# A two-stage layer on one core: small weight parts, a reordered last step, transposes in pairs, last product by halves

## The reference

```python
x = x + attn(layernorm(x))   # proj = x @ W_in * mup; conv over 4 tokens, silu; scan:
    state = state * dA_t + (dt_t * x_t) * B_t ;  y_t = state . C_t
    g = (y + D * x) * silu(z);  g = g * rsqrt(mean(g^2) + eps) * norm_w;  out = g @ W_out
x = x + ffn(layernorm(x))    # g = (x @ gate_w.T) * gate_s; u = (x @ up_w.T) * up_s
    out = ((silu(g) * u) @ down_w.T) * down_s
```

## Time and profile before

| | |
|---|---|
| median of 3 runs | 789.67 us (788.21 to 789.69) |
| the profiled execution | 788.09 us, its span 786.2 us |
| TensorE matmuls busy | 741.8 us (94%) |
| VectorE, ScalarE, POOL busy | 517.7, 494.7, 291.3 us |
| DMA busy (mean of 16 engines) | 41.6% for the program's own queue |
| first stage | 0 to about 523 us |
| second stage | about 526 us to the end |

### The profile page before, as it was taken

How to read it: one execution, slowest core, us unless ns; L and a number is a source line. 1 busy time by engine, 2 the same in 40 slices (tenths; PEclk the granted TensorE clock), 3 DMA queues, 4 the chain that set the end, 5 groups by cost and what they waited for, 6 DMA issues and landing times.

```text
span 786.2 us, 20260 instructions
## 1 busy us (share of the span) xinstructions
PE 741.8 (94%) x8464; PEld 609.7 (78%) x8464; DVE 517.7 (66%) x843; ACT 494.7 (63%) x941; POOL 291.3 (37%) x232
## 2 busy tenths in 40 slices
PE   4877999999999999999999999779999999999997
PEld 4865888888887887887887887567878878887886
DVE  6978976886886887788797796845424532632331
ACT  5988888978977978978978878723312321321330
POOL 2163285375466446546636717420010011001002
PEclk9988999999999999999999999999999999999999
DMA  9833243484484375266367284784013013002002
GB/s 296 232 82 88 47 101 109 100 233 124 83 239 134 85 197 176 79 152 218 84 146 208 71 214 119 254 289 155 0 55 108 0 43 118 0 14 93 0 1 82
DMA packets 42025, 94.94 MB, mean 121 GB/s; under 512 B 9744, under 2 KB 15376, under 8 KB 41744
## 3 DMA queue, kind: packets, MB, share of 16 engines
q1 hardware_dynamic: 41936, 93.67, 41.6%
HBM read 84.73 MB, written 17.57 MB: 130 GB/s over the span
## 4 chain that ended last, share of the span: by engine, by line
PE 51%; DVE 22%; ACT 13%; DMA 6%; issue 5%; POOL 2%; SPq 1%; POOLq 0%; DVEq 0%; ACTq 0%
PE ps_y L1591 10%; DVE cx L895 9%; PE ps_proj L1578 8%; PE ps_out L1578 5%; PE ps_x L1578 5%; PE ps_proj L1174 3%; PE ps_proj L1175 3%; PE ps_proj L1176 3%; ACT ring L678 3%; PE ps_x L1223 3%; DVE ring L950 3%; PE ps_y L1246 2%; DVE dt_p L870 2%; DVE state L960 2%; ACT sz L621 2%
## 5 line engine op out<-in xcount | busy, mean ns | idle before, releaser
L507 POOL TENSOR_TENSOR ring<-tokd,ring 128x1024 f32<-128x1024 f32 x64 | 122.2, 1923 | 187.4 <-ACT tokd L673 125.5
L1174 PE MATMUL ps_proj<-xn_hi,win_hi 128*128 128x256 f32 x608 | 179.0, 294 | 2.7 <-DVE xn_lo L864 2.7
L1175 PE MATMUL ps_proj<-xn_lo,win_hi 128*128 128x256 f32 x608 | 172.9, 284 | 0.0
L1176 PE MATMUL ps_proj<-xn_hi,win_lo 128*128 128x256 f32 x608 | 172.6, 284 | 0.0
L1174 PEld LDWEIGHTS ps_proj<-xn_hi,win_hi 128*128 128x128 f32 x608 | 116.7, 192 | 17.3 <-issue 11.4
L1175 PEld LDWEIGHTS ps_proj<-xn_lo,win_hi 128*128 128x128 f32 x608 | 116.9, 192 | 0.3
L1176 PEld LDWEIGHTS ps_proj<-xn_hi,win_lo 128*128 128x128 f32 x608 | 116.8, 192 | 0.0
L895 DVE SCALAR_TENSOR_TENSOR cx<-cin,consts,cx 128x256 f32<-128x256 f32 x240 | 96.4, 483 | 0.0
L1469 POOL TENSOR_TENSOR res<-res,hidden 128x512 f32<-128x512 f32 x16 | 20.5, 1282 | 184.0 <-DVE hidden L1532 184.0
L950 DVE TENSOR_TENSOR ring<-ring,ps_tok 128x1024 f32<-128x1024 f32 x64 | 75.7, 1215 | 4.2 <-ACT ring L682 4.2
L678 ACT ACTIVATE ring<-ring 128x1024 f32<-128x1024 f32 x64 | 66.7, 1058 | 10.3 <-POOL ring L507 10.3
(11 more groups left out here) (164 smaller groups left out, 1638.1 us busy)
## 6 DMA issues: line engine op xcount, KB each, us to landing
ring<-cum_dram SPq DMA_DIRECT2D x128, 256.0 KB, 5.1
xin<-x SPq DMA_DIRECT2D x8, 512.0 KB, 3.8
res<-x SPq DMA_DIRECT2D x32, 128.0 KB, 2.7
x_dram<-res SPq DMA_DIRECT2D x32, 128.0 KB, 3.2
x_in_sb<-x_dram SPq DMA_DIRECT2D x4, 1024.0 KB, 6.3
res<-x_dram SPq DMA_DIRECT2D x16, 256.0 KB, 2.7
out<-res SPq DMA_DIRECT2D x16, 256.0 KB, 2.0
gate_w_copy<-gate_w SPq DMA_DIRECT2D x4, 704.0 KB, 6.7
```

The costliest lines, as they stand in the source:

```text
L507: pool.tensor_tensor(ring[:, g, :, :], own, ring[:, g, :, :], ALU.subtract).then_inc(diffed, 1)
L1174: pe.matmul(out, win_hi[:, k, cols], xn_hi[:, k, :], start=(k == 0), stop=False)
L1175: pe.matmul(out, win_hi[:, k, cols], xn_lo[:, k, :], start=False, stop=False)
L1176: made = pe.matmul(out, win_lo[:, k, cols], xn_hi[:, k, :], start=False, stop=(k == KT - 1))
```

## The change

1. The weights land in 27 parts: `wg` and `wu` in 8 parts of 352 KB each (128 rows of 704 columns), `wd` in 11 parts of 256 KB. Two on their way at a time as before, and the x1 stores still behind the last part.
2. Tiles 0 and 1 of the first x1 block are loaded one block of the first stage earlier, into the mixer's `xin`, ahead of two weight copies; their statistics and normalisation stand in step 14, their transposes in step 15 right behind `turn_x`.
3. The last step is reordered: `gate_lo(14)` behind `make_xpad`, `scale_carry` ahead of `mix(15, 0)`, the last `skip` made on POOL instead of ScalarE.
4. In `finish` the transposes go in two pairs, one behind t = 0 and one behind t = 1; VectorE's `norm_lo` follows in pairs.
5. The very last tile's product is made in two column halves into two banks; the second half is scaled and added on VectorE (POOL keeps the first) and each half is stored by itself.

```diff
@@ -60,7 +60,8 @@
 BT = 512
 NB = BATCH * LEN // BT
 TT = BT // P
-WEIGHT_PARTS = 2 * KT + 4
+HALF_N = INTER // 2
+WEIGHT_PARTS = 4 * KT + MT
 LOW_WIDTHS = (1024, 1024, 768)
 LOW_EACH = 2 * len(LOW_WIDTHS)
 LOW_PARTS = 3 * LOW_EACH
...
@@ -388,9 +388,11 @@
 
             def body(i, first, last):
                 if i - 1 in LOOKED:
+                    sp.wait_ge(hand.low_max_made, 3 * (i - 2) + 1)
                     if i + 1 < BLOCKS:
-                        sp.wait_ge(hand.low_max_made, 3 * (i - 2) + 1)
                         load_x(i + 1)
+                    else:
+                        sp.dma_start(xin[:], hand.x1_by_block[0, :, 0:2, :]).then_inc(hand.first_in, 16)
                     keep_weights(2 * (i - 2))
                     keep_weights(2 * (i - 2) + 1)
                 if not first:
@@ -432,20 +434,18 @@
                 body(i, False, False)
             body(BLOCKS - 1, False, True)
             sp.wait_ge(projected, EVENTS * BLOCKS)
-            sp.dma_start(hand.xin[:], hand.x1_by_block[0]).then_inc(hand.x_in, 16)
+            sp.dma_start(hand.xin[:, 2:TT, :], hand.x1_by_block[0, :, 2:TT, :]).then_inc(hand.x_in, 16)
             sp.wait_ge(hand.weights_kept, 16 * COPIES)
 
             def load_weights(n):
 
                 if n >= 2:
                     sp.wait_ge(hand.weights_in[n % 2], 16 * (n // 2))
-                if n < KT:
-                    to, part = hand.wg[:, n, :], hand.gate_t[:, n, :]
-                elif n < 2 * KT:
-                    to, part = hand.wu[:, n - KT, :], hand.up_t[:, n - KT, :]
+                if n < 4 * KT:
+                    k, of = n % (2 * KT) // 2, slice(n % 2 * HALF_N, (n % 2 + 1) * HALF_N)
+                    to, part = (hand.wg, hand.wu)[n // (2 * KT)][:, k, of], (hand.gate_t, hand.up_t)[n // (2 * KT)][:, k, of]
                 else:
-                    of = hand.down_parts[n - 2 * KT]
-                    to, part = hand.wd[:, of, :], hand.down_t[:, of, :]
+                    to, part = hand.wd[:, n - 4 * KT, :], hand.down_t[:, n - 4 * KT, :]
                 sp.dma_start(to.bitcast(F32), part).then_inc(hand.weights_in[n % 2], 16)
 
             load_weights(0)
...
@@ -550,6 +564,10 @@
                         fade_state(i, j)
                     if j == 0 and not last:
                         norm_scale(i + 1)
+                    elif j == 0:
+                        mlp_scale(0)
+                    if closing:
+                        last_skip()
                     if not closing:
                         for g in range(GROUPS):
                             if g == GROUPS - 1 and not opening:
@@ -566,11 +584,7 @@
             for i in range(1, BLOCKS - 1):
                 body(i, False, False)
             body(BLOCKS - 1, False, True)
-            pool.wait_ge(hand.zeroed, 2)
-            pool.wait_ge(hand.moments_made, TT)
-            pool.tensor_tensor(hand.spread[:], hand.moments[:, :, 1], hand.eps[:], ALU.add).then_inc(hand.eps_added, 1)
-            pool.wait_ge(hand.eps_added, 1)
-            pool.tensor_tensor(hand.rstd[:], hand.spread[:], hand.minus_half[:], ALU.pow).then_inc(hand.rstd_made, 1)
+            mlp_scale(1)
             fold_squares(STEPS * BLOCKS - 1)
             rms_scale(STEPS * BLOCKS - 1, 1)
             mlp.gpsimd(pool)
...
@@ -751,10 +770,13 @@
                 c = STEPS * i + 1
                 keep_tok(c)
                 fade(c, 0)
-                square(c - 1)
-                if not last:
+                if last:
+                    clamp(c, 2)
+                    square(c - 1)
+                else:
+                    square(c - 1)
                     evacuate(i + 1, 1)
-                clamp(c, 2)
+                    clamp(c, 2)
                 fade(c, 1)
                 if not last:
                     evacuate(i + 1, 2)
@@ -764,8 +786,11 @@
                 if not last:
                     evacuate(i + 1, 3)
                     first_taps(i + 1, CONV_ORDER[0:2])
-                make_skip(i, 1)
-                if not last:
+                if last:
+                    mlp_norm_hi(0)
+                    mlp_norm_hi(1)
+                else:
+                    make_skip(i, 1)
                     first_taps(i + 1, CONV_ORDER[2:4])
                     first_taps(i + 1, CONV_ORDER[4:6])
                     make_run(i + 1)
...
@@ -1010,6 +1028,10 @@
                 if first:
                     weight_lo(EVENTS)
                 update_state(c, 0)
+                if last:
+                    mlp_stats(0)
+                    mlp_normalise(0)
+                    mlp_normalise(1)
                 if first:
                     weight_lo(EVENTS + 1)
                 if not last:
@@ -1027,25 +1049,25 @@
                     all_low_max()
 
                 c = STEPS * i + 1
-                gate_lo(c - 1)
                 if last:
                     mask_cb(c)
                     make_xpad(i, 1)
+                    gate_lo(c - 1)
                     make_x1(c - 2)
-                    mix(c, 0)
-                    mlp_stats()
                     scale_carry(i, 1)
-                    for g in range(1, GROUPS):
+                    for g in range(GROUPS):
                         mix(c, g)
                     make_y(c)
                     gate(i, 1)
-                    mlp_normalise(0)
-                    mlp_normalise(1)
+                    mlp_stats(1)
                     gate_lo(c)
+                    mlp_norm_lo(0)
+                    mlp_norm_lo(1)
                     mlp_normalise(2)
                     mlp_normalise(3)
                     any_low()
                     return
+                gate_lo(c - 1)
                 for n in range(1, 4):
                     soft(i + 1, n)
                 mask_cb(c)
...
@@ -1319,6 +1354,9 @@
                 if not last:
                     project(i + 1, 1)
                 turn_x(i, 1)
+                if last:
+                    mlp_turn(0)
+                    mlp_turn(1)
                 if not last:
                     project(i + 1, 2)
                 carry(i, 1)
...
+                    store_half(j, 0)
+                    store_half(j, 1)
+                else:
+                    store(j, TT - 1)
 
             def store(j, t):
                 sp.wait_ge(out_ready, AHEAD + TT * j + t + 1)
                 sp.dma_start(out_by_block[bass.ds(j, 1), :, t, :].rearrange("a p h -> (a p) h"), res[:, t % 2, :]).then_inc(stored[t % 2], 16)
+
+            def store_half(j, n):
+                t, cols = TT - 1, half_cols(n)
+                if n == 0:
+                    sp.wait_ge(out_ready, AHEAD + TT * j + t + 1)
+                else:
+                    sp.wait_ge(half_ready, 1)
+                sp.dma_start(out_by_block[j, :, t, cols], res[:, t % 2, cols]).then_inc(stored[t % 2], 16)
 
             body(0, True, False)
             with sp.Fori(1, NB - 1) as j:
                 body(j, False, False)
...
@@ -1530,6 +1575,21 @@
                 if t >= 2:
                     dve.wait_ge(out_ready, AHEAD + TT * j + t - 1)
                 dve.tensor_tensor(hidden[:, t % 2, :], ps_o[t % 2], scale_d[:], ALU.mult).then_inc(down_scaled, 1)
+
+            def scale_down_half(j, n):
+
+                t, cols = TT - 1, half_cols(n)
+                dve.wait_ge(down_made, TT * j + t + 1 + n)
+                if n == 0:
+                    dve.wait_ge(out_ready, AHEAD + TT * j + t - 1)
+                made = dve.tensor_tensor(hidden[:, t % 2, cols], ps_last[n], scale_d[:, cols], ALU.mult)
+                if n == 0:
+                    made.then_inc(down_scaled, 1)
+                    return
+                made.then_inc(half_scaled, 1)
+                dve.wait_ge(half_scaled, 1)
+                dve.wait_ge(res_in[t % 2], 16 * (2 * j + t // 2 + 1))
+                dve.tensor_tensor(res[:, t % 2, cols], res[:, t % 2, cols], hidden[:, t % 2, cols], ALU.add).then_inc(half_ready, 1)
 
             def body(j, first, last):
                 for m in range(MT):
...
@@ -1549,12 +1609,19 @@
                         normalise(j + 1)
                 dve.wait_ge(h_split, MT * j + MT)
                 scale_down(j, 0)
+                if not last:
+                    norm_lo(j + 1, 0)
+                    norm_lo(j + 1, 1)
                 scale_down(j, 1)
                 if not last:
-                    for t in range(TT):
-                        norm_lo(j + 1, t)
+                    norm_lo(j + 1, 2)
+                    norm_lo(j + 1, 3)
                 scale_down(j, 2)
-                scale_down(j, 3)
+                if last:
+                    scale_down_half(j, 0)
+                    scale_down_half(j, 1)
+                else:
+                    scale_down(j, 3)
 
             body(0, True, False)
             with dve.Fori(1, NB - 1) as j:
...
@@ -1605,18 +1683,25 @@
             def finish(j, last, exact):
                 pe.wait_ge(h_split, MT * j + MT - 2)
                 down(j, 0, exact)
```

(17 more changed lines are left out.)

92 lines of the change are left out of this document (57 added, 35 removed).

## The result

The changed kernel takes 796.01 us (median of 6 runs, 794.54 to 797.94), the kernel before 788.58 beside it (785.59 to 789.69). The ratio is 1.0103, with a 95% interval of 1.0075 to 1.0131: slower, as forecast, by 7.4 us instead of 3.4, inside the range. The profiled execution took 794.66 with a span of 793.0, against 788.09 and 786.2.

The account below looks back on a forecast made before the run. The hand-over was taken to be bound by how fast SP gets through its list, x1 stores last. Pair 5 +6.6, clock +1.8, transposes -3.1, halves -1.1 on 788.09, plus 0.8 towards the median, gave 793.1 us, range 787.0 to 799.0.

Parts of the forecast that it names:

- the sum: Total against the profiled execution of 788.09: + 6.6 + 1.8 - 3.1 - 1.1 = + 4.2 us.
- the round trips: SP's weight list: each 352 KB part takes r1 = 3.0 us, each 256 KB part r2 = 2.6; bounds 2.4 to 3.5 and 3.0.
- the start of the list: SP: step 13's store lands by 503.1, so weight part 2 is issued at about 504.4 instead of 507.91, 3.5 us earlier.
- over 6 as its sign: Sign that the forecast is right: VectorE waits over 6 us for the second x1 block.
- Early tiles 0 and 1 ... Cost 0: Steps 14 and 15: their work, under 3 us, fits VectorE's 4.59 us wait for PE, transposes PE's wait for `xpad`; cost 0.
- Last step ... gains nothing: Reordered last step: PE ends the first stage 3 to 4 us sooner, about 519.5, but waits for weights until 525.9.
- Clock: PE behind its 7.3 us standstill before pair 5: matmuls at the lower clock cost +1.8 us; bounds 0 and 2.0.
- Transposes: Second stage, transposes in pairs: all 3.2 us of PE's waits go, less 0.1 for more changes: -3.1 us.
- Halves: Last product in two halves: work behind the last matmul shrinks from 2.03 to 1.0 us, quicker half store: -1.1 us.
- The last step late as well: Slower rival: ring loads behind a load and two copies make step 15 1.6 us later, 794.7 us; chance 0.13.
- The small parts at the large parts' rate: Faster rival: round trips shrink with size to 2.4 and 1.8 us, pair 5 at 544.6, total 783.1; chance 0.20.
- the case in between: No-change rival: round trips of 2.7 and 2.5 us and a clock that stays up, 788.7 us; chance 0.17.

Follow-up runs that it names:

- e2: The kernel before with nothing but the 27 small weight parts: 801.36 us, ratio 1.0176.
- e3: The changed kernel, small parts kept, with the x1 stores and the second x1 load ahead of the parts of `wd`: 787.50 us, ratio 1.0012.
- e4: The changed kernel with four small parts on their way instead of two: 780.03 us, ratio 0.9910.
- e12: e10 with the last product still by halves but stored once, in whole rows: 780.01 us, ratio 0.9896.
- e7: e1 with GpSimd held until VectorE's normalisations of the first two and last two rows are done: 779.11 us, ratio 0.9914.
- e1: The changed kernel with the twelve large weight parts of before, all else kept: 779.02 us, ratio 0.9905.
- e11: e10 with GpSimd held by the two waits of e7: 776.12 us, ratio 0.9856.
- e10: Changed kernel, twelve large parts: two before step 13's store, six of `wg`/`wu` at once behind the residual load, x1 stores and load before `wd`: 775.72 us, ratio 0.9857.
- e13: e11 with 48 increments of an unused semaphore on SP behind the last residual load: 775.86 us, ratio 0.9854.
- e6: e1 without the last product by halves (scaled, added and stored whole, as before): 782.45 us, ratio 0.9940.
- e5: The kernel before with only the second stage's transposes in pairs: 782.70 us, ratio 0.9953.

## Why the prediction was right or wrong

*Right: what bounds the kernel, and by what mechanism.* The hand-over hung on SP's list, small parts lengthened it, the x1 stores and pair 5 came late, the clock fell. e2, e3 and e4 show each link. From the issue of part 26 to pair 5 I had 14.4 us, it was 14.3.

*In the range, in part by luck.* From +0 on the sum had +4.2 and the profiles differ by +9.9. That the spans differ by only 6.8 is due to the 3.1 us ahead of +0, which the change doesn't explain.

*Mis-sized: the round trips.* This is the step of the sum that failed most. "I take r1 = 3.0 and r2 = 2.6"; measured 3.44 and 2.80. That is 7 x 0.44 + 5 x 0.20 = 4.1 us. I took the duration of loads alone and a reading of the large parts that split their time into a fixed 1.3 and a share by size. With two on their way the fixed share is larger: from 704 KB (4.8) to 352 KB (3.44) only 1.4 is saved, so on a straight line through these two sizes 2.1 stay whatever the size (an estimate). The upper bound of 3.5 came from 512 KB and would have been the better guide. The Trainium skill's fixed part ("DMA: Bandwidth & Descriptors", § Anatomy of one DMA) is 2.0, near this 2.1, but its sum, 2.8 and 2.6, falls short of both measurements; the measurement decides. The page has its figures from transfers issued by GpSimd, and these are issued by SP.

*Mis-sized: the start of the list.* Forecast 3.5 earlier than before, measured 2.1 (+25.8 for part 2, before +27.9). Step 13's store was issued 0.9 later than I assumed. From its landing to part 2 I had 503.1 to 504.4, 1.3 us, where the row before gives 1.7 (506.2 to 507.91), and it was 1.9. The list's start and the round trips together are 1.4 + 4.1 = 5.5 us; pair 5 came 5.3 later than forecast. The wait moved as well: the second stage began 5.7 later than forecast (+52.5 instead of +46.8), so that PE stood for 4.5 before pair 5 instead of 7.3, and VectorE waited 5.3 for the second x1 block, where the prediction named over 6 as its sign.

*Wrong: "Early tiles 0 and 1 ... Cost 0".* They fit the wait of VectorE, but not beside GpSimd's `diff`, which stood in that wait too. The second state update came at +12.8 instead of +12.0, and at +14.3 where the `diff` was first (e3, e12). In the changed kernel this 0.8 is part of the store's 0.9. In a run in which the parts don't hide it, the last matmul starts 1.9 us sooner with GpSimd held (e7 against e1) and 0.7 sooner (e11 against e10). These are single profiles: e13, which is e11 but for the 48 increments, is 0.9 sooner than e11.

*"Last step ... gains nothing": not refuted.* The first stage was to end 3 to 4 us sooner. It ends 2.6 sooner in the changed kernel (+40.7 instead of +43.3), where 11.8 us of wait cover it, 3.0 sooner in e6, and 0.5 sooner in e1 (+42.8), where the clock is low in step 15; but e5, whose first stage is that of the kernel before, ends it 1.7 later (+45.0), so single profiles say little here. e1, with the old parts, is 7.4 us faster than before, where I had expected 6. In its profile the pairs give 4.2 and the halves 1.6, and pair 5 comes 1.1 sooner. Part 2 is issued 2.2 sooner there (+25.7 instead of +27.9), and PE still waits 2.5 for the weights before the second stage, so the 1.1 goes with the list, and nothing shows that the last step gave it. No run changes the last step alone.

*Clock: right in size.* From pair 5 to the last matmul the changed kernel takes 232.5 against 230.9 in e1: 1.6 us for the clock, forecast 1.8 (e2 against before: 1.5). The forecast was made for a standstill of 7.3 us and the one that came was 4.5, so that the sizes agree says little for its working. The standstill before the second stage cost a slow start as well (granted 0.54 and 0.77), hidden behind the wait for pair 5.

*Transposes: mechanism right, size off.* Forecast -3.1, measured -4.3.

*Halves: wrong.* "-1.1 us". The work behind the last matmul did get shorter, by the forecast amount (from 2.1 to 0.9 us), but the end of the program came 0.5 later. The term left out is an instruction packet that goes ahead of a sixteenth of the last store. Where it doesn't (e1, e10) the halves give 1.6, of which 0.3 is the half store's quicker landing. I had no row for how a change of the code moves an instruction fetch into the last microseconds.

*The rivals.* "The last step late as well" was half right: a delay of step 15 did appear, not through the order of the ring loads on SP (the `diff` started as early as before), but through the ports. The small parts at the large parts' rate (2.4 and 1.8) and the case in between (2.7 and 2.5) are out by the measured 3.44 and 2.80, and by e1 and e2.

## What to carry to other kernels

Cut a transfer that is waited for into smaller parts only if as many more may be on their way at once: with a fixed number in flight the list costs parts times round trip, here about 2 us of it fixed. Order the list by who is waiting, and put nothing late behind a long chain (e3 took 7 us out by order alone). Work moved into an engine's idle time has to be checked against its neighbours' work too, VectorE against GpSimd above all, and a gain at the very end against the last store's landing, not the last instruction.

## What was not expected of the hardware

- A `tensor_scalar` of 128x512 f32 on VectorE takes 0.50 us alone and 2.12 when it starts behind a GpSimd `tensor_tensor` of 1.9 us. Which comes first differs between nearly equal programs: step 15's second state update starts at +11.9 to +12.2 with no `diff` beside the tiles (e4, e7, e11, e13), at +12.6 to +12.8 with VectorE first, at +14.3 with the `diff` first (e3, e12).
- PE's wait of 1.07 us in a dense stream costs 1.42.
- One 16 KB packet of an instruction fetch (0.9 to 1.6 us long) held up a sixteenth of the last store in eight kernels, and the end came 1.4 to 2.4 us later than where the packet came behind the store.
- After waits of 2.0 to 2.8 us in step 15 the first `ps_out` matmul took 0.79 in e1 and e7 and 0.80 in e4 (lower clock), and 0.50 in the changed kernel, e6 and the kernel before. Equal waits are followed by either level; what decides between them isn't shown here.
